# Two more tables taken by one-hot matmul in a recommendation tower: eleven tables and 60 gathers in place of nine and 68

## What is computed

```python
e = jnp.stack([tbl_0[ids[:, 0]], ..., tbl_25[ids[:, 25]]], axis=1)
combined = jnp.concatenate([dense[:, None, :], e], axis=1)          # (512, 27, 128)
interactions = jnp.einsum('bfd,bgd->bfg', combined, combined)
z = jnp.concatenate([dense, interactions[:, iu, ju]], axis=1)       # upper triangle, 351 pairs
h = jnp.concatenate([z, dense], axis=1)
h = jnp.maximum(h @ W_top1 + b_top1, 0.0)                           # 607 -> 512
h = jnp.maximum(h @ W_top2 + b_top2, 0.0)                           # 512 -> 256
y = h @ W_top3                                                      # 256 -> 1
```

## Time and profile before

| | us |
|---|---|
| median of 3 runs (lowest, highest) | 160.23 (157.64, 160.42) |
| the profiled execution | 156.5 |
| its span, first to last instruction | 154.7 |
| busy: PE, DVE, ACT, POOL | 117.9, 74.1, 73.0, 68.4 |
| mean granted clock of TensorE | 0.901 |
| moved by DMA | 12.58 MB |

### The profile page before, as it was taken

How to read it: one execution, slowest core, us unless ns; L and a number is a source line. 1 busy time by engine, 2 the same in 40 slices (tenths; PEclk the granted TensorE clock), 3 DMA queues, 4 the chain that set the end, 5 groups by cost and what they waited for, 6 DMA issues and landing times.

```text
span 154.7 us, 2685 instructions
## 1 busy us (share of the span) xinstructions
PE 117.9 (76%) x1038; PEld 98.9 (64%) x1038; DVE 74.1 (48%) x153; ACT 73.0 (47%) x160; POOL 68.4 (44%) x75
## 2 busy tenths in 40 slices
PE   0689999985979967550595728489929989799994
PEld 0446776662756856540394628478829989798993
DVE  3499999999999960407204510030505020237000
ACT  6795994995897820426104522002505313236211
POOL 2648072260345747474447465446456474100000
PEclk9999999999999999776559997865985799999999
DMA  5828765487961011111112121111121111100000
GB/s 156 222 71 267 207 190 110 160 221 199 354 181 42 17 51 38 34 51 34 39 44 52 28 63 32 49 34 38 34 51 33 39 50 25 27 6 0 4 0 1
DMA packets 6304, 12.58 MB, mean 81 GB/s; under 512 B 2545, under 2 KB 3157, under 8 KB 6163
## 3 DMA queue, kind: packets, MB, share of 16 engines
q1 hardware_dynamic: 3971, 7.68, 17.2%
q0 software_dynamic: 2176, 4.46, 10.9%
q10 hardware_dynamic: 144, 0.26, 0.8%
HBM read 11.27 MB, written 0.00 MB: 73 GB/s over the span
## 4 chain that ended last, share of the span: by engine, by line
DMA 34%; PE 27%; POOL 24%; issue 13%; DVE 1%; ACT 1%
DMA rows<-in_tbl_dram,ids_i 31%; POOL rows L343 24%; PE ps L603 12%; PE ps L574 7%; PE ps L525 2%; PE ps L616 2%; DMA ids_i<-in_ids_dram 2%; PE ps L558 2%; DVE z L488 1%; PE ps L626 1%; PE ps L624 1%; ACT emb_t L403 0%; DVE h_t L497 0%; ACT y L430 0%
## 5 line engine op out<-in xcount | busy, mean ns | idle before, releaser
L343 POOL DMA_INDIRECT rows<-in_tbl_dram,ids_i x68 | 67.6, 994 | 63.0 <-DMA rows<-in_tbl_dram,ids_i 45.2
L461 DVE TENSOR_SCALAR hot<-ps,row_no 125x512 fp32r<-125x512 f32 x54 | 36.6, 739 | 1.0 <-PE ps L512 1.0
L488 DVE COPY z<-ps 32x112 f32<-32x112 f32 (+1 forms) x64 | 16.5, 258 | 34.9 <-PE ps L574 22.7
L574 PE MATMUL ps<-emb_t 128*64 128x52 f32 x512 | 23.6, 251 | 11.8 <-issue 8.3
L574 PEld LDWEIGHTS ps<-emb_t 128*64 128x64 f32 x512 | 21.1, 166 | 14.8 <-issue 11.3
L542 PE MATMUL ps<-hot,tab_hi 125*128 125x512 f32 x72 | 30.0, 416 | 0.8 <-issue 0.8
L411 ACT COPY z<-ps 32x112 f32<-32x112 f32 (+1 forms) x64 | 15.2, 238 | 30.8 <-PE ps L574 19.7
L545 PE MATMUL ps<-hot,tab_lo 125*128 125x512 f32 x72 | 29.1, 404 | 0.7 <-DVE tab_lo L450 0.7
L558 PE MATMUL ps<-ident,rows 128*128 128x128 f32 x68 | 12.0, 304 | 15.2 <-DMA rows<-in_tbl_dram,ids_i 9.7
L558 PEld LDWEIGHTS ps<-ident,rows 128*128 128x128 f32 x68 | 8.3, 153 | 18.3 <-DMA rows<-in_tbl_dram,ids_i 11.7
L542 PEld LDWEIGHTS ps<-hot,tab_hi 125*128 125x128 f32 x72 | 14.1, 196 | 5.5 <-issue 2.4
(11 more groups left out here) (44 smaller groups left out, 92.7 us busy)
## 6 DMA issues: line engine op xcount, KB each, us to landing
tab<-in_tbl_dram SPq DMA_DIRECT2D x9, 448.0 KB
rows<-in_tbl_dram,ids_i POOLq DMA_INDIRECT x68, 4.6
w_fold<-w_pair SPq DMA_DIRECT2D x1, 1024.0 KB
w<-in_W_top_dram SPq DMA_DIRECT2D x1, 512.0 KB, 5.1
tab<-in_tbl_dram SPq DMA_DIRECT2D x9, 52.0 KB
x_rows<-in_r_dense_features_dram ACTq DMA_DIRECT2D x1, 256.0 KB, 3.2
w_x<-in_W_top_dram SPq DMA_DIRECT2D x1, 256.0 KB
h_t<-in_W_top_dram SPq DMA_DIRECT2D x1, 256.0 KB
```

Of the source, the lines that this page charges most:

```text
L343: pool.indirect_dma_start(out=rows[:, t, gathered.index(f), :], out_offset=None, in_=tables[f - 1], in_offset=bass.IndirectOffsetOnAxis(id ...
L461: nc.vector.tensor_scalar(hot[0:RP, k % OHB], ps[0:RP, IDV + n % 2, :], row_no[0:RP, c:c + 1], None, ALU.is_equal).then_inc(hot_dve, 1)
L488: last = nc.vector.tensor_copy(dst, src)
L574: last = nc.tensor.matmul(ps[32 * q:32 * (q + GT), bank, col:col + GC], emb_t[:, t, b0:b0 + GT, :].rearrange("p b f -> p (b f)"), emb_t[:, ...
```

## The change

Features 9 and 19 (tables of 1250 rows) leave the gathers and become the last two one-hot features. Their tables fill the same 125 partitions with ten rows each, so they have ten chunks, of which ACT makes 2, 5 and 8. A second set of row numbers (10p+c) is made for them, the table buffers grow from eight to ten chunks, and what counted in eights now counts with `chunks_to`, `act_to` and `dve_to`. In ACT's `build_hots` the two activations are interleaved, since `away` has two buffers and there may now be three chunks. The remaining 15 gathered features are in four groups a tile: three and the dense vector, four, four, four. The order of steps changes with them: group 0 of tile 1 stands between the one-hot features, and the last four one-hot features have no other group between them. On SP the tables 9 and 10 are loaded behind table 8 and ahead of the ten pieces of `w_fold`.

```diff
@@ -13,10 +13,10 @@
 SLOTS = 32
-ONEHOT = [4, 10, 11, 16, 17, 18, 22, 25, 26]
-
-
-GROUPS = [[(0, 4)], [(12, 4)], [(5, 4)], [(9, 1), (19, 3)], [(23, 2)]]
+ONEHOT = [4, 10, 11, 16, 17, 18, 22, 25, 26, 9, 19]
+
+
+GROUPS = [[(0, 4)], [(12, 4)], [(5, 4)], [(20, 2), (23, 2)]]
 def features(group):
...
@@ -27,11 +27,11 @@
 ORDER = [
-    "h h g0:0 h g1:0 h g2:0 h g3:0 h g4:0 h h h",
-    "u0:0 g0:1 u1:0 g1-4:1 u0-1:1",
-    "g0-1:2 x0 l0-1:0 g2:2 l2-3:0 g3:2 e0 g4:2 y0",
+    "h h g0:0 h g1:0 h g2:0 h g3:0 h h g0:1 h h h h",
+    "u0:0 g1:1 u1:0 g2-3:1 u0-1:1",
+    "g0-1:2 x0 l0-1:0 g2:2 l2-3:0 g3:2 e0 y0",
     "u0:2 x1 l0:1 u1:2 l1-3:1 g0:3 e1 g1:3 y1",
-    "x2 l0-1:2 g2:3 l2-3:2 g3-4:3 u0:3 x3 u1:3 e2 l0-1:3 y2 l2-3:3 e3 y3",
+    "x2 l0-1:2 g2:3 l2-3:2 g3:3 u0:3 x3 u1:3 e2 l0-1:3 y2 l2-3:3 e3 y3",
 ]
...
@@ -73,17 +73,35 @@
     NH = len(ONEHOT)
     R8 = 8
     RP = tables[ONEHOT[0] - 1].shape[0] // R8
+    CHUNKS = [tables[f - 1].shape[0] // RP for f in ONEHOT]
+    MAXC = max(CHUNKS)
     NG = len(GROUPS)
     NPAIR = NF * (NF - 1) // 2
     ND = 2
-    ACT_CHUNKS = (3, 6)
-    DVE_CHUNKS = tuple(c for c in range(R8) if c not in ACT_CHUNKS)
+    ACT_CHUNKS = [(3, 6) if m == R8 else (2, 5, 8) for m in CHUNKS]
+    DVE_CHUNKS = [tuple(c for c in range(m) if c not in a) for m, a in zip(CHUNKS, ACT_CHUNKS)]
     OHB = 10
     RAW = 2
     SPLIT = 2
     gathered = [f for g in GROUPS for f in features(g) if f]
     assert D == P and N1 == BK and sorted(gathered + ONEHOT) == list(range(1, NF))
-    assert all(tables[f - 1].shape[0] == R8 * RP for f in ONEHOT) and w1.shape[0] == 2 * D + NPAIR
+    assert all(tables[f - 1].shape[0] == m * RP for f, m in zip(ONEHOT, CHUNKS)) and w1.shape[0] == 2 * D + NPAIR
+    assert set(CHUNKS) == {R8, MAXC}
+
+    def chunks_to(n):
+
+        return sum(CHUNKS[:n])
+
+    def act_to(n):
+        return sum(map(len, ACT_CHUNKS[:n]))
+
+    def dve_to(n):
+        return sum(map(len, DVE_CHUNKS[:n]))
+
+    def row_cols(n, c):
+
+        at = c if CHUNKS[n] == R8 else R8 + c
+        return slice(at, at + 1)
     steps = plan_steps()
...
@@ -93,7 +111,7 @@
         return banked.index(s) % 2
     def stored_by_act(s):
-        return s[0] == "hot" or s[2] in ((1, 3, 4) if s[1] == 0 else (0, 2, 4))
+        return s[0] == "hot" or s[2] in ((1, 3) if s[1] == 0 else (0, 2))
     def stored_count(s):
         return sum(stored_by_act(b) == stored_by_act(s) for b in banked[:banked.index(s) + 1])
...
@@ -273,9 +291,9 @@
                 if n >= RAW:
                     sp.wait_ge(lo_ready, n - RAW + 1)
-                lines = tables[ONEHOT[n] - 1].rearrange("(p c) d -> p c d", c=R8)
+                lines = tables[ONEHOT[n] - 1].rearrange("(p c) d -> p c d", c=CHUNKS[n])
                 for p0, p1 in ((0, SPREAD), (SPREAD, RP)):
-                    sp.dma_start(tab[p0:p1, n % RAW], lines[p0:p1]).then_inc(tab_in[n], 16)
+                    sp.dma_start(tab[p0:p1, n % RAW, 0:CHUNKS[n]], lines[p0:p1]).then_inc(tab_in[n], 16)
             def load_pairs(first, last):
                 for i in range(first, last):
...
@@ -304,7 +322,8 @@
             load_table(7)
             sp.wait_ge(w_pair_in, 16 * (NCOL + 1))
             sp.dma_start(w_fold[:], w_pair[:, 0:KF, :]).then_inc(w_fold_in, 16)
-            load_table(8)
+            for n in range(8, NH):
+                load_table(n)
             sp.wait_ge(w_fold_in, 16)
             for i in range(4 * KF, NCOL):
                 k, at = fold_to(i)
...
@@ -356,22 +376,27 @@
             def split_hi(n):
                 act.wait_ge(tab_in[n], 32)
                 if n >= SPLIT:
-                    act.wait_ge(hot_used, (n - SPLIT + 1) * R8)
-                nc.scalar.copy(tab_hi[0:RP, n % SPLIT], tab[0:RP, n % RAW]).then_inc(hi_ready, 1)
+                    act.wait_ge(hot_used, chunks_to(n - SPLIT + 1))
+                nc.scalar.copy(tab_hi[0:RP, n % SPLIT, 0:CHUNKS[n]], tab[0:RP, n % RAW, 0:CHUNKS[n]]).then_inc(hi_ready, 1)
             def build_hots(n):
                 act.wait_ge(ids_bc_act, n + 1)
                 if n == 0:
                     act.wait_ge(row_no_ready, 1)
-                for m, c in enumerate(ACT_CHUNKS):
-                    a = n * len(ACT_CHUNKS) + m
+
+                def how_far(m):
+                    a = act_to(n) + m
                     if a >= 2:
                         act.wait_ge(hot_act, a - 1)
                     nc.scalar.activation(away[0:RP, a % 2], ps[0:RP, IDA + n % 2, :], ACT.Abs,
-                                         bias=neg_row[0:RP, c:c + 1]).then_inc(away_ready, 1)
-                for m, c in enumerate(ACT_CHUNKS):
-                    a = n * len(ACT_CHUNKS) + m
-                    k = n * R8 + c
+                                         bias=neg_row[0:RP, row_cols(n, ACT_CHUNKS[n][m])]).then_inc(away_ready, 1)
+
+                how_far(0)
+                for m, c in enumerate(ACT_CHUNKS[n]):
+                    if m + 1 < len(ACT_CHUNKS[n]):
+                        how_far(m + 1)
+                    a = act_to(n) + m
+                    k = chunks_to(n) + c
                     act.wait_ge(away_ready, a + 1)
                     if k >= OHB:
                         act.wait_ge(hot_used, k - OHB + 1)
...
@@ -447,18 +472,19 @@
             def split_lo(n):
                 dve.wait_ge(hi_ready, n + 1)
-                nc.vector.tensor_tensor(tab_lo[0:RP, n % SPLIT], tab[0:RP, n % RAW], tab_hi[0:RP, n % SPLIT].bitcast(F32),
-                                        ALU.subtract).then_inc(lo_ready, 1)
+                full = slice(0, CHUNKS[n])
+                nc.vector.tensor_tensor(tab_lo[0:RP, n % SPLIT, full], tab[0:RP, n % RAW, full],
+                                        tab_hi[0:RP, n % SPLIT, full].bitcast(F32), ALU.subtract).then_inc(lo_ready, 1)
             def build_hots(n):
                 dve.wait_ge(ids_bc_dve, n + 1)
-                for m, c in enumerate(DVE_CHUNKS):
+                for m, c in enumerate(DVE_CHUNKS[n]):
                     if m == 2:
                         split_lo(n)
-                    k = n * R8 + c
+                    k = chunks_to(n) + c
                     if k >= OHB:
                         dve.wait_ge(hot_used, k - OHB + 1)
-                    nc.vector.tensor_scalar(hot[0:RP, k % OHB], ps[0:RP, IDV + n % 2, :], row_no[0:RP, c:c + 1],
+                    nc.vector.tensor_scalar(hot[0:RP, k % OHB], ps[0:RP, IDV + n % 2, :], row_no[0:RP, row_cols(n, c)],
                                             None, ALU.is_equal).then_inc(hot_dve, 1)
             build_hots(0)
...
@@ -533,17 +559,17 @@
                     wait_bank(s)
                     pe.wait_ge(hi_ready, n + 1)
                     bank = ps[:, ROT + bank_of(s), :]
-                    for c in range(R8):
-                        if c in ACT_CHUNKS:
-                            pe.wait_ge(hot_act, n * len(ACT_CHUNKS) + ACT_CHUNKS.index(c) + 1)
+                    for c in range(CHUNKS[n]):
+                        if c in ACT_CHUNKS[n]:
+                            pe.wait_ge(hot_act, act_to(n) + ACT_CHUNKS[n].index(c) + 1)
                         else:
-                            pe.wait_ge(hot_dve, n * len(DVE_CHUNKS) + DVE_CHUNKS.index(c) + 1)
-                        one_hot = hot[0:RP, (n * R8 + c) % OHB]
+                            pe.wait_ge(hot_dve, dve_to(n) + DVE_CHUNKS[n].index(c) + 1)
+                        one_hot = hot[0:RP, (chunks_to(n) + c) % OHB]
                         nc.tensor.matmul(bank, tab_hi[0:RP, n % SPLIT, c], one_hot, start=c == 0, stop=False)
                         if c == 0:
                             pe.wait_ge(lo_ready, n + 1)
                         nc.tensor.matmul(bank, tab_lo[0:RP, n % SPLIT, c], one_hot,
-                                         start=False, stop=c == R8 - 1).then_inc(hot_used, 1)
+                                         start=False, stop=c == CHUNKS[n] - 1).then_inc(hot_used, 1)
                     if n + 2 < NH:
                         broadcast_ids(n + 2)
                 elif s[0] == "group":
...
```

27 lines of the change are left out of this document (14 added, 13 removed).

## The result

| | before | changed |
|---|---|---|
| median of 4 runs, us (lowest, highest) | 158.95 (157.64, 160.42) | 144.15 (143.07, 145.31) |
| changed to before, 95% interval | | 0.912 (0.894 to 0.930) |
| the profiled execution, us | 156.5 | 145.31 |
| its span, us | 154.7 | 143.1 |
| mean granted clock | 0.901 | 0.952 |

The ratio of 0.912 compares the faster executions of each kernel (the medians alone would give 0.907), and the profiled execution of the changed kernel is the longest of its four.

The account below looks back on a forecast made before the run. Bound by the serial string of gathers, with DVE's one-hot stage in front of every Gram. 11.0-5.4-6.3-0.7+0.4-4.6 = -5.6 gave 150.9 of the profiled 156.5, by ratio 154.5 from a median of 160.23; range 148 to 162.

Parts of the forecast that it names:

- the string: GpSimd's serial groups of gathers, each issued after the one before landed: last landing at 115.8 to 122.3 instead of 133.5.
- The one-hot stage: Start to first Gram unit: two ten-chunk tables more on DVE, +11.0 us (10.5 to 12.5), first Gram at 68.4.
- the slower rival: PE falls to half clock inside the two long one-hot tables and becomes the bound: +3.5, by ratio 163.8 us; chance 0.10.
- First Gram to tile 1's: From the first Gram unit to tile 1's: the new order of steps saves 3.5 to 7.3 us, taken as -5.4.
- the stops: PE's unexplained gaps at Gram units, such as 1.08 us before 63.84: untouched by the change and left in.
- late z copy: Tile 0's z copies on DVE start 3.8 us after their Gram's last record; prompt copies would make -5.4 into -7.3.
- Waits for rows: PE's waits of 3.57, 1.98 and 0.77 us behind tile 1's stage all go: -6.3, at worst -4.3.
- The clock: Half-clock stretches behind the waits, 94.60 to 98.00 and 101.40 to 108.25, run at full clock: -4.6, lower bound 0.
- the first rival: Stops and late z copies go too, until the string may hold PE: priced at -11, 149.0 us; chance 0.21.
- the clock does not come back: Stops stay and keep the stretches at half clock, z copies are late: +1.0, by ratio 161.3 us; chance 0.27.

Follow-up runs that it names:

- a_again: The changed kernel, unchanged, run again on chip C: 155.72 us, beside 157.36 of the kernel before.
- a_pad16: The changed kernel with 16 tiny matmuls ahead of PE's first work, on chip B: 142.70 us, ratio 0.912 to the kernel before.
- a_pace2: The changed kernel with GpSimd's waits between gather groups kept in tiles 0 and 1 alone, on chip B: 137.15 us, ratio 0.876 to the kernel before.
- a_hot9: The changed kernel without the one-hot work of features 9 and 19, on chip B: 140.41 us against 158.51 of the kernel before, ratio 0.896.
- b_shift32: The kernel before with 32 small matmuls ahead of PE's first work, on chip A: 157.22 us against 155.53, ratio 1.008.
- a_third: The changed kernel, unchanged, run once more on chip D: 157.10 us, beside 156.44 of the kernel before.
- b_pace1: The kernel before with GpSimd's waits between gather groups kept in tile 0 alone: 134.07 us on chip B (ratio 0.856), 184.63 on chip D (1.177).
- b_again: The kernel before, unchanged, run again on chip C: 156.60 us, ratio 1.001.

## Why the prediction was wrong

**What bounds the kernel: right, and then left out of the sum.** I wrote that more than half of the chain is the string, that it ends at 133.55, and that PE is at the last group at 133.62. (The row of 133.62 holds the last two groups; the last itself begins near 134.1, half a us behind its landing.) Two chains that meet within half a us are both bounds. Yet I made the sum on PE's alone and let the string stand by ("It does not set the end by itself: PE must come to it"). That is true only if PE is the later one. In the changed kernel it is the other way round on the chip of the result: the last group is transposed at 120.52 after a wait of 0.42 us for its rows. This caps the gain rather than explains it, since PE had to gain 13 us to be held at all. The string's own arithmetic was good: I had 115.8 to 122.3 for its last landing. Its stages: tile 0's gathers end at 39.03 (38.30), tile 1 takes 30.4 (27.1 and the disturbance of loads and splits that I had priced beside it), tile 2 25.3 and tile 3 25.8 (25.2).

**The one-hot stage: the size right, its place in the sum wrong.** +11.0 with bounds 10.5 to 12.5; the first Gram unit stands at 68.71 in a_again, 69.49 in a_pad16 and 70.42 in a_pace2, 11.3, 12.1 and 13.0 later than the earlier trace rows (the last two with one or two slices of the clock line below full in that stage). DVE's turn is 6.02, as worked out. The 71.38 of the profiled execution has a stretch at half clock more, from 37.7 to 44.6, in which DVE waits for PE; that is a smaller case of the slower rival, in the short tables rather than in the long ones, which ran at full clock. But in series the 11 us are not: a_hot9 leaves them out and gains 2.3; b_shift32 adds 10 of them and loses 1.7.

**First Gram to tile 1's, and the Gram stages of tiles 1 and 2: this is the step that failed.** These three stages were forecast at about -6.4 and measured -24.2. In the first I had -5.4, "the middle" between a late and a prompt z copy, and of the stops "The change doesn't touch them, and I leave both in". Measured: -11.2, then -5.9 up to x0 where I had 0, and -7.1 up to x2 where I had about -1. In the changed kernel's profile both, stops and late copies, are gone. The change did not remove them, though: they are there in a_again and a_third and missing in b_pace1 and a_pad16: they go with the chip. Where they stay, the first stage comes out as forecast: 12.1 us in a_again against 18.3 in b_again, -6.3. The profile of before came from an execution with them and the result from a chip without them. From one profile that could not be known; that an idle "for nothing that the profile names" isn't a property of the program was to be suspected, and the late z copy had no cause in the trace either (ACT's copies of the same unit start at 70.49 as well, so that PE's signal comes late rather than DVE). My own case against the rival, that a stop also stood in tile 0's unit "so they recur with the code", was wrong in the inference.

**Waits for rows: right in size on the wrong kind of chip.** Without stops PE is faster than the string, and 3.62 and 0.42 us of wait remain where I had none. With stops (a_again, a_third) there is none behind the first Gram unit, as forecast.

**The clock and the stages behind it: half right, and the other half mis-sized.** Of my 4.6 the first part did not come: in place of 94.60 to 98.00 there is a stretch at half clock from 95.8 to 99.2, behind the wait of 3.62 us. The rest came, and with it what I had left in: from tile 2's first Gram unit to x2 the kernel takes 13.0 for 20.2. The missing 7.1 are the stops of the second unit (2.8), half of the cold stretch behind them (3.0) and half of what stood at half clock up to 108.25 (1.2). Half clock is still there at the last group, 123.1 to 126.5, behind two waits; this is the tail's +1.5. All of these stretches stand behind an idle PE. The Trainium skill (TensorE: Matmul & The Clock Gate, "HAM oscillation — how this bites in real kernels") has the rule: a long enough pause between groups of matmuls makes the next one start cold. The trace agrees in the main, but the last pause alone doesn't decide it: behind 2.56 us of idle the two Gram units of 79.70 ran at full clock (3.94 us), behind 0.42 and 1.27 us that of 122.45 did not (3.18).

**The rivals.** What happened is the first rival's course, by another cause (it had the program's new points and fewer gathers remove the stops, but they went with the chip): stops and late copies gone, PE "would then reach the last group at 120.2, where the string may hold it"; measured 120.52, held for 0.42. Its price of -11 on the profiled 156.5 gives 145.5; the profiled execution took 145.31. That these agree within 0.2 is in part luck: the price stood near the string's upper end, 122.3, and the string came 1.8 us sooner, while the tail took 1.5 more. I gave it 0.21. Its 149.0 for the median was still 4.9 too high, because I carried one execution with stops over by the ratio 160.23/156.5 to a median that seems to come from a chip without them; why the kernel before takes no less there (158.5 to 159.0) isn't shown. On chips with stops the outcome is the third case, "the clock does not come back", or the lower edge of the forecast: the profiled a_again took 152.35 against 150.9 forecast, and in the medians 155.72 against 157.36 and 157.10 against 156.44 are nearer to nothing than to my -5.6. The slower rival's mechanism did not appear in the long tables.

**Where the gain comes from,** then: in the two profiles the kernels end 21.1 and 22.6 us after PE reaches the last rows of the string, and the change brings that point 13.1 us forward (133.62 to 120.52), of which the tail gives 1.5 back in a stretch at half clock. PE can follow only where nothing stops it; on a chip with stops PE, with 11 us more in front of it, becomes the bound and takes nearly all of it back. The first profile is of the kind with stops and the second without, so that the 13.1 are read across the two kinds; b_shift32, a_hot9 and b_pace1, each on one chip, bear out that the string and not DVE's work sets the pace.

**What stays open.** What holds PE: neither a running issue nor a running transfer alone, since it was held 7.7 us beyond the last issue and with no packet moving. Whether it happens in an execution that isn't recorded: every execution here has its span and clock on record. What tells the chips apart, and whether it is the chip or the session. Why the late z copy comes with the stops. No version was found that wins everywhere: b_pace1 (0.856) and a_pace2 (0.876) beat both kernels on chips without stops and lose 18% and 11% to the kernel before on chip D. The changed kernel was never clearly slower than the kernel before, and 9% faster on the chip of the result.

## What to carry to other kernels

When two chains reach the same step within a microsecond, work out the end of each and take the later; a sum of gains and losses along one of them is no forecast. An idle time for which the profile names nothing is no term that stays or goes with an edit: run the unchanged kernel again, on another chip, before any of it is priced. And test a version that issues many indirect DMAs back to back on more than one chip, since a gain of 14% on one was a loss of 18% on the next.

## What the runs showed of the hardware

- PE can be held while GpSimd issues indirect DMAs, by the chip or the session: 43 matmul records in 40 us against 453 in the same program (184.63 against 134.07 us), and for 6.3 us more in which no DMA packet moved. The records stand at multiples of 0.70 us; in ordinary paced runs it shows as stops of up to 1.1 us in the Gram units.
- A gather takes GpSimd 0.94 us and 0.30 to the next; beside a split of two inputs on DVE it took 1.70 to 1.81 (58.49 above), 2.11 in the earlier trace rows.
- 32 fp32 matmuls with 128 rows and only 8 columns took 13.82 us in b_shift32 (64 records): 0.43 a matmul, the same as the distance between two one-hot matmuls of 512 columns (fp32r, one record each) in the earlier trace rows. The 16 small matmuls of a_pad16, with weights of 32x8 in place of 128x128, took 0.95 us together, 0.06 each: here the weights set the cost, not the columns.
